# The first two tiles are only centred, their deviation moves behind the first product, and two context loads wait for gathered rows

## The chip, the core and the metric

The kernel runs on one core of a Trainium2 chip. Five engines work side by side, each through its own list of instructions in order: TensorE (PE in the profile) for matrix products, VectorE (DVE), ScalarE (ACT), GpSimd (POOL) and SyncE (SP), which here only issues transfers. The metric is the device time of one execution in microseconds, as the median of several runs: 421.14 us before (three runs, 420.02 to 422.06). All cores but one are idle, so the slowest core is the only one.

## The reference

`x` has 2048 rows (tokens) of 512. Two sub-layers follow each other:

```python
x = x + tanh(g_xattn) * moe(layernorm(x), token_ids, ctx, ctx, ctx)
x = x + tanh(g_ffn)   * ffn(layernorm(x), w_gate, w_up, w_down)
# moe: expert = min(clip(id, 0, 24999) // 6250, 3); per token, with C = ctx[expert] (512 x 512)
#      h = x @ C.T ; y = (silu(h) * h) @ C        (Wg, Wu and Wd are one and the same matrix)
# ffn: int8 activations, ternary weights, silu(gate) * up, a Walsh-Hadamard transform of 2048,
#      int8 again, and the product with w_down
# layernorm(x) = (x - mean) / sqrt(var + 1e-5), without weights
```

Because a row is only scaled by its deviation, `layernorm(x) @ C.T` is `((x - mean) @ C.T) * rstd`, where `rstd` is 1 / sqrt(var + 1e-5). The change rests on that.

## The kernel before

Tokens are sorted by expert. 16 tiles of 128 sorted rows are gathered from `x` by indirect transfers into `xs`; a tile that holds rows of two experts is computed once for each, so there are 19 items. An item goes through: `stats` (mean and variance, VectorE), `item_scale` (two GpSimd instructions: variance plus epsilon, then the power -1/2), `normalise` (VectorE, into `xn`), `x_transposes` (TensorE), `x_upper` and `x_lower` (the transposed tile is split in a high and a low part, ScalarE and VectorE), `up_product` (12 matmuls of high and low parts), `silu_h` (ScalarE), `act_mul` (VectorE), `a_transposes`, `a_upper` and `a_lower` (the same split), `down_product` (12 matmuls) and `update` (VectorE adds into `xs`). The context matrices are split too: `ct_upper(e)` on ScalarE and `ct_lower(e)` on VectorE, each over 128 x 2048. The first two items (`k < FIRST`, FIRST is 2) do without the split in the up product: `first_product` multiplies whole float32 values of `stage`, the buffer into which the four context matrices are loaded.

Beside the items, the weights of the second sub-layer are loaded into the same four slots of `stage` (`W_DRAM`, L258 to L265), measured, rounded and clipped. A quarter of the first weight matrix may be loaded once `ct_lower` of that slot is done and both first products are. After the items come 16 feed-forward tiles, from about 150 us on, in a software pipeline.

The order on every engine is written out by hand, and waits are on semaphores that count. For the first items it is:

- SP: constants, three context loads at once, the fourth (`e == E - 1`, L254) when the second gathered tile is in (`gathered[1]`), then the weights.
- POOL: gathers 0 to 2, `item_scale(0)`, `item_scale(1)`, gathers 3 to 6, `item_scale(2)`, `item_scale(3)`, gathers 7 to 10, and so on (L325 to L337). A gather's descriptors are made by GpSimd, so each gather occupies it.
- DVE (L1094 to L1115): the list that the change reorders; it is printed below.
- ACT: `ct_upper` of 0, 1 and 2, `x_upper(0)`, `x_upper(1)`, `ct_upper(3)`, `silu_h(0)`, `a_upper(0)`, then item by item.
- PE (L501 to L511): `spin` (matmuls whose result nobody reads, so that TensorE isn't idle), `x_transposes(0)`, `first_product(0)` with `x_transposes(1)` in its middle, `first_product(1)` with `a_transposes(0)` in its middle, `x_transposes(2)`, `down_product(0)`, `a_transposes(1)`, and then for every item k from 2: `up_product(k)`, `x_transposes(k + 1)`, `down_product(k - 1)`, `a_transposes(k)`.

`xn` has two buffers (`b = k % 2`), `item_rstd` and `item_mv` too; `sil`, `act`, `ps_aT` and `aT_hi`/`aT_lo` have one.

Of the kernel before, what the change touches and what calls it, by code (L numbers as in the profile page):

```python
# [75 lines left out]
def gated_moe_bitnet_kernel(nc, x, ids, ctxt, wgate, wup, wdown, gates, consts, out):  # L76
    with ExitStack() as persistent:
# [29 lines left out]
        item_rstd = sb("item_rstd", [P, 2], F32)  # L107
        ffn_stats = sb("ffn_stats", [P, 2, 6], F32)
# [106 lines left out]
        tables_set, tanh_done = sem("tables_set"), sem("tanh_done")  # L215
        ct_hi_set, ct_lo_set = sem("ct_hi_set"), sem("ct_lo_set")
# [31 lines left out]
        def _(sp):  # L248
# [4 lines left out]
            for e in range(E):  # L253
                if e == E - 1:  # L254
                    sp.wait_ge(gathered[1], 16)
                sp.dma_start(stage[:, e, :], ctxt[:, e, :]).then_inc(in_slot[e], 16)
# [45 lines left out]
        def _(pool):  # L302
# [11 lines left out]
            def item_scale(k, n):  # L314
# [6 lines left out]
                nc.gpsimd.tensor_tensor(item_rstd[:, b:b + 1], item_var[:, b:b + 1], neg_half[:, :],  # L321
# [98 lines left out]
        def _(pe):  # L420
# [44 lines left out]
            def first_product(k, between=None):  # L465

                e = expert_of(k)
                pe.wait_ge(ct_hi_set, e + 1)
# [32 lines left out]
            spin(18)  # L501
            pe.wait_ge(stats_set, 1)
            spin(5)
            x_transposes(0, 0)
            spin(4)
# [200 lines left out]
        def _(act_e):  # L706
# [20 lines left out]
            def silu_h(k):  # L727
                act_e.wait_ge(h_done, k + 1)
                nc.scalar.activation(sil, (first_h[k] if k < FIRST else ps_h)[:, :], ACT.Silu).then_inc(sil_set, 1)
# [20 lines left out]
            for e in range(E - 1):  # L750
                ct_upper(e)
            x_upper(0, 0)
            x_upper(1, 1)
            ct_upper(E - 1)
            silu_h(0)
            a_upper(0)
# [22 lines left out]
            for k in range(1, NI):  # L779
                w, i = k // 5, k % 5  # L780
                silu_h(k)
                if k + 1 < NI:
                    x_upper(k + 1, 1 - k % 2)
# [159 lines left out]
        def _(dve):  # L943
# [132 lines left out]

            def x_lower(k, b):
                dve.wait_ge(xT_hi_set, k + 1)
                tt(xT_lo[:, :], ps_xT[:, :], xT_hi[:, :].bitcast(F32), ALU.subtract).then_inc(xT_lo_set, 1)

            def act_mul(k):
                dve.wait_ge(sil_set, k + 1)
                tt(act, (first_h[k] if k < FIRST else ps_h)[:, :], sil, ALU.mult).then_inc(act_set, 1)
# [11 lines left out]
            stats(0, 0, st)  # L1095
            dve.wait_ge(gathered[1], 16)
            stats(1, 1, st)
            normalise(0, 0)
            normalise(1, 1)
            ct_lower(0)  # L1100
            ct_lower(1)
            act_mul(0)
            dve.wait_ge(gathered[2], 16)
            stats(2, 0, st)
            a_lower(0)
            normalise(2, 0)
            dve.wait_ge(gathered[3], 16)
            stats(3, 1, st)
# [392 lines left out]
```

## Time and profile before

| what | value |
|---|---|
| median of three runs | 421.14 us |
| lowest and highest | 420.02 and 422.06 us |
| the profiled execution's own time | 422.38 us |
| its span in the profile | 420.4 us |
| busy: PE, DVE, ACT, POOL | 390.6 us (93%), 365.4 us (87%), 291.2 us (69%), 178.7 us (43%) |
| first 20 us: PE, DVE, POOL busy | 9.88, 12.82, 6.04 us |
| 50 to 130 us: PE busy | 79.45 of 80 us |
| granted TensorE clock, mean | 0.996 |

The span is the time from the first to the last instruction of the profiled execution; the 1.98 us between it and that execution's time lie outside what the profile shows. TensorE is busy 93% of the span, and nearly all of the time from 50 to 130 us. In the first 20 us it is busy for less than half, and much of that are spins. So the start is a stretch with another limit than the rest. In the rows further below, L numbers are lines of the kernel before; `bank` is a PSUM bank; "scratch" stands for `xn`, `sil` or `act`, which are parts of it; `wq` in the first 30 us is where the whole transposed first tiles lie (`xT_whole`).

### The profile page before, as it was taken

The page shows a single profiled execution, that of the slowest core. Times are in us where ns is not written, and L with a number is a line of the kernel's source. Part 1 is how long each engine was busy: PE and PEld are TensorE (multiplying, and loading weights), DVE is VectorE, ACT ScalarE, POOL GpSimd, SP SyncE. Part 2 cuts the span into 40 slices and gives each one's busy share as a digit, 9 for nine tenths or more (in the row PEclk, how much of TensorE's full clock was granted, in tenths as well). Part 3 has the DMA queues.
Part 4 walks back from the last instruction along what each step waited for, and adds up shares of the span by engine and source line. Part 5 has one row for each costly group of instructions (what it writes and reads, how often), then busy time and mean ns, then how long its engine had stood idle before and what let it go on. Part 6 is the DMA issues. An engine that isn't in the chain of part 4 may idle for free.

```text
span 420.4 us, 7393 instructions
## 1 busy us (share of the span) xinstructions
PE 390.6 (93%) x2203; PEld 270.0 (64%) x2203; DVE 365.4 (87%) x652; ACT 291.2 (69%) x450; POOL 178.7 (43%) x208
## 2 busy tenths in 40 slices
PE   1899999999999999988999999999999999999891
PEld 0347788888887664755666666666666666667740
DVE  5788587679885889999999999999999999998980
ACT  4446686687784343667878878878878878877960
POOL 0667311014123202174475575575575575522021
PEclk9999999999999999999999999999999999999998
DMA  7759474065000001336255245255155155155241
GB/s 257 251 160 410 157 247 154 1 212 189 2 13 2 0 14 38 39 62 90 50 101 126 49 103 126 46 108 125 42 112 125 38 112 125 39 113 114 50 101 50
DMA packets 48968, 43.66 MB, mean 104 GB/s; under 512 B 42672, under 2 KB 42800, under 8 KB 46896
## 3 DMA queue, kind: packets, MB, share of 16 engines
q1 hardware_dynamic: 44224, 27.11, 23.4%
q0 software_dynamic: 4720, 16.26, 16.3%
q8 instruction: 13, 0.21, 0.2%
q14 instruction: 11, 0.09, 0.1%
HBM read 21.33 MB, written 4.19 MB: 61 GB/s over the span
## 4 chain that ended last, share of the span: by engine, by line
PE 77%; DVE 11%; issue 5%; DMA 4%; ACT 1%; POOL 0%; DVEq 0%; SPq 0%; POOLq 0%; ACTq 0%
PE bank L461 21%; PE bank L584 12%; PE bank L591 11%; PE bank L560 10%; PE bank L567 10%; PE bank L423 9%; DVE prod L1174 2%; DVE mixed L1201 1%; DVE ct_lo L964 1%; DMA xqT<-xq 1%; DMA xs<-x_dram,order 1%; PE bank L528 1%; DVE prod L1201 1%; PE bank L677 1%; DMA yqT<-yq 1%
## 5 line engine op out<-in xcount | busy, mean ns | idle before, releaser
L584 PEld LDWEIGHTS bank<-cst,mT 128*128 128x128 f32 x512 | 66.3, 191 | 14.1 <-issue 2.7
L584 PE MATMUL bank<-cst,mT 128*128 128x128 f32 x512 | 67.8, 276 | 4.0 <-ACT mT L829 4.0
L560 PE MATMUL bank<-wq,xqT 128*128 128x512 bf16 x240 | 61.6, 379 | 1.7 <-DMA xqT<-xq 1.7
L591 PE MATMUL bank<-wq,yqT 128*128 128x512 bf16 x240 | 61.3, 379 | 0.7 <-DMA yqT<-yq 0.7
L567 PE MATMUL bank<-wq,xqT 128*128 128x512 bf16 x240 | 61.6, 379 | 0.0
L829 ACT ACTIVATE mT<-bank 128x512 f32<-128x512 f32 x64 | 37.6, 592 | 18.4 <-PE bank L423 18.4
L406 POOL DMA_INDIRECT out_dram<-res,order x16 | 19.5, 1217 | 70.8 <-DVE res L1295 70.8
L817 ACT ACTIVATE y<-y,yqs 128x512 int8<-128x512 f32 x56 | 40.2, 717 | 9.9 <-POOL yqs L366 9.9
L854 ACT ACTIVATE sg<-bank,gate_s 128x512 f32<-128x512 f32 x60 | 41.0, 683 | 7.4 <-PE bank L560 7.2
L1174 DVE TENSOR_TENSOR prod<-bank,sg 128x512 f32<-128x512 f32 x64 | 43.4, 677 | 1.1 <-ACT sg L854 0.8
L834 ACT ACTIVATE y<-bank 128x512 f32<-128x512 f32 x64 | 37.6, 588 | 8.8 <-PE bank L584 8.6
L567 PEld LDWEIGHTS bank<-wq,xqT 128*128 128x128 bf16 x240 | 23.5, 98 | 28.3
L423 PE MATMUL bank<-cst,mixed 128*128 128x128 f32 x256 | 37.9, 273 | 0.2 <-DVE mixed L1193 0.2
L1274 DVE TENSOR_REDUCE ymax_part<-y 128x1 f32<-128x1024 f32 x30 | 36.3, 1211 | 2.1 <-ACT y L834 1.1
L423 PEld LDWEIGHTS bank<-cst,mixed 128*128 128x128 f32 x256 | 31.5, 141 | 10.2 <-issue 0.4
L1201 DVE TENSOR_TENSOR mixed<-prod 128x1024 f32<-128x1024 f32 x32 | 37.9, 1219 | 0.1
L1201 DVE TENSOR_TENSOR prod<-bfly 128x1024 f32<-128x1024 f32 x30 | 36.0, 1211 | 0.0
L822 ACT ACTIVATE yq<-y 128x512 bf16<-128x512 int8 x56 | 35.2, 629 | 0.6
L1201 DVE TENSOR_TENSOR bfly<-prod 128x1024 f32<-128x1024 f32 x30 | 35.3, 1217 | 0.0
L364 POOL TENSOR_SCALAR out_s<-yamax,down_c 128x1 f32<-128x1 f32 x13 | 28.6, 2197 | 15.6 <-DVE yamax L1285 15.6
L560 PEld LDWEIGHTS bank<-wq,xqT 128*128 128x128 bf16 x240 | 23.1, 98 | 18.3 <-issue 2.7
L591 PEld LDWEIGHTS bank<-wq,yqT 128*128 128x128 bf16 x240 | 23.1, 98 | 17.2 <-DMA yqT<-yq 1.1
(154 smaller groups left out, 810.2 us busy)
## 6 DMA issues: line engine op xcount, KB each, us to landing
mixed<-mixed POOLq DMA_DIRECT2D x15, 512.0 KB, 5.3
stage<-ctx_dram SPq DMA_DIRECT2D x4, 1024.0 KB, 7.5
stage<-wgate_dram SPq DMA_DIRECT2D x4, 1024.0 KB, 8.5
stage<-wup_dram SPq DMA_DIRECT2D x4, 1024.0 KB, 4.7
stage<-wdown_dram SPq DMA_DIRECT2D x4, 1024.0 KB, 4.7
yqT<-yq SPq DMA_TRANSPOSE x60, 2.4
cst<-consts_dram SPq DMA_DIRECT2D x1, 274.0 KB, 3.3
xs<-x_dram,order POOLq DMA_INDIRECT x16, 4.2
```

The costliest lines, as they stand in the source:

```text
L423: last = nc.tensor.transpose(bank_[:, c * P:(c + 1) * P], src(c), ident)
L461: last = nc.tensor.matmul(bank_[:, :], l[:, cols], r[:, ds(e * DC + c), :], start=(c == 0 and n == 0), stop=(c == DC - 1 and n == 2))
L560: last = nc.tensor.matmul(ps_gate[:, :], xqT[:, b, c, :], wq[:, 0, c * F + 512 * n:c * F + 512 * (n + 1)], start=(c == 0), stop=(c == DC - 1))
L567: last = nc.tensor.matmul(ps_up[n % 2][:, :], xqT[:, b, c, :], wq[:, 1, c * F + 512 * n:c * F + 512 * (n + 1)], start=(c == 0), stop=(c == ...
L584: last = nc.tensor.matmul(bank_[:, c * P:(c + 1) * P], mT[:, n % 2, c, :], had, start=True, stop=True)
L591: last = nc.tensor.matmul(ps_down[b][:, :], yqT[:, m, g, :], wq[:, 2, block_ * D:(block_ + 1) * D], start=(m == 0 and g == 0), stop=(m == ...
L817: nc.scalar.activation(y8[:, m % 2, :], y[:, b, 512 * m:512 * (m + 1)], ACT.Copy, scale=yqs[:, b:b + 1]).then_inc(yround_set, 1)
L829: nc.scalar.activation(mT[:, n % 2, :, :].rearrange("p c m -> p (c m)"), ps_mT[n % 2][:, :], ACT.Copy).then_inc(mT_set, 1)
L834: nc.scalar.activation(y[:, b, 512 * n:512 * (n + 1)], bank_[:, :], ACT.Copy).then_inc(y_set, 1)
L854: nc.scalar.activation(sg[:, n % 2, :], ps_gate[:, :], ACT.Silu, scale=gate_s[:, b:b + 1]).then_inc(sg_set, 1)
L1174: tt(prod[:, b, 4 * n:4 * n + 4, :].rearrange("p c m -> p (c m)"), up[n % 2][:, :], sg[:, n % 2, :], ALU.mult).then_inc(prod_set, 1)
L1201: return tt(dst[:, :, half], src[:, :, 0], src[:, :, 1], ALU.subtract if half else ALU.add)
```

## The change

- `normalise(0)` and `normalise(1)` are replaced by `centre(0)` and `centre(1)`, which subtract the mean and wait for no deviation. The deviation (now in a buffer of its own, `first_rstd`) is applied as the scale of the Silu and as a scalar in `act_mul`, of the first two items only. `centre(0)` now stands before `stats(1)`.
- On VectorE, `stats(2)` moves ahead of `act_mul(0)`, `normalise(2)` ahead of `a_lower(0)`, and `ct_lower(1)` from before `act_mul(0)` to between `normalise(2)` and `a_lower(0)`. Two waits for `rstd_set` are added ahead of `stats(2)` and `stats(3)`.
- The third context matrix is loaded when the first gathered tile is in, the fourth when the third is.
- On ScalarE, a new semaphore `ctx_in` tells TensorE that a context matrix has arrived. `ct_upper(2)` moves from before `x_upper(0)` to behind `silu_h(0)`, and `ct_upper(3)` from before `silu_h(0)` to behind `x_upper(2)`; ScalarE waits for both arrivals before `silu_h(0)`.
- The spins: 18, a wait for the first statistics, 5 and 4 become 20 and 3.
- The GpSimd order stays as it was.

```diff
--- before.py
+++ after.py
@@ -251,8 +253,10 @@
             sp.dma_start(cst[:, C_RANK:C_N], consts[:, C_RANK:C_N]).then_inc(in_small, 16)
             sp.dma_start(gate_in[:, :], gates).then_inc(in_gate, 16)
             for e in range(E):
-                if e == E - 1:
-                    sp.wait_ge(gathered[1], 16)
+                if e == 2:
+                    sp.wait_ge(gathered[0], 16)
+                if e == 3:
+                    sp.wait_ge(gathered[2], 16)
                 sp.dma_start(stage[:, e, :], ctxt[:, e, :]).then_inc(in_slot[e], 16)
 
             for w in range(3):
@@ -318,7 +322,8 @@
                 nc.gpsimd.tensor_scalar(item_var[:, b:b + 1], item_mv[:, b, 1:2], 1.0, LN_EPS, ALU.mult,
                                         ALU.add).then_inc(pool_step, 1)
                 pool.wait_ge(pool_step, n + 1)
-                nc.gpsimd.tensor_tensor(item_rstd[:, b:b + 1], item_var[:, b:b + 1], neg_half[:, :],
+                rstd = first_rstd if k < FIRST else item_rstd
+                nc.gpsimd.tensor_tensor(rstd[:, b:b + 1], item_var[:, b:b + 1], neg_half[:, :],
                                         ALU.pow).then_inc(rstd_set, 1)
                 return n + 1
 
@@ -465,7 +470,7 @@
             def first_product(k, between=None):
 
                 e = expert_of(k)
-                pe.wait_ge(ct_hi_set, e + 1)
+                pe.wait_ge(ctx_in, e + 1)
                 pe.wait_ge(xT_hi_set, k + 1)
                 for c in range(DC):
                     if c == DC // 2 and between is not None:
@@ -498,11 +503,9 @@
                 pe.wait_ge(aT_lo_set, k + 1)
                 product(bank_, aT_hi[:, :], aT_lo[:, :], e, y_done)
 
-            spin(18)
-            pe.wait_ge(stats_set, 1)
-            spin(5)
+            spin(20)
             x_transposes(0, 0)
-            spin(4)
+            spin(3)
             pe.wait_ge(tables_set, 1)
             first_product(0, lambda: x_transposes(1, 1))
             first_product(1, lambda: a_transposes(0))
@@ -726,7 +729,12 @@
 
             def silu_h(k):
                 act_e.wait_ge(h_done, k + 1)
-                nc.scalar.activation(sil, (first_h[k] if k < FIRST else ps_h)[:, :], ACT.Silu).then_inc(sil_set, 1)
+                if k < FIRST:
+                    act_e.wait_ge(rstd_set, k + 1)
+                    nc.scalar.activation(sil, first_h[k][:, :], ACT.Silu,
+                                         scale=first_rstd[:, k:k + 1]).then_inc(sil_set, 1)
+                else:
+                    nc.scalar.activation(sil, ps_h[:, :], ACT.Silu).then_inc(sil_set, 1)
 
             def a_upper(k):
                 act_e.wait_ge(aT_done, k + 1)
@@ -747,12 +755,20 @@
                 nc.scalar.activation(w8(w, c), stage[:, c, :], ACT.Copy,
                                      scale=wscale[:, w:w + 1]).then_inc(wround_set, 1)
 
-            for e in range(E - 1):
+            def ctx_arrived(e):
+
+                act_e.wait_ge(in_slot[e], 16)
+                nc.scalar.nop().then_inc(ctx_in, 1)
+
+            for e in range(2):
+                ctx_arrived(e)
                 ct_upper(e)
             x_upper(0, 0)
             x_upper(1, 1)
-            ct_upper(E - 1)
+            ctx_arrived(2)
+            ctx_arrived(3)
             silu_h(0)
+            ct_upper(2)
             a_upper(0)
 
             def ln_normalise(t, b):
@@ -779,7 +795,10 @@
             for k in range(1, NI):
                 w, i = k // 5, k % 5
                 silu_h(k)
-                if k + 1 < NI:
+                if k == 1:
+                    x_upper(2, 0)
+                    ct_upper(3)
+                elif k + 1 < NI:
                     x_upper(k + 1, 1 - k % 2)
                 if w < 3 and i in (2, 3):
                     weight_abs(w, 2 * i - 3)
@@ -1074,13 +1093,20 @@
                 ts(xn[:, b, :], rows(tau), item_mv[:, b, 0:1], item_rstd[:, b:b + 1], ALU.subtract,
                    ALU.mult).then_inc(xn_set, 1)
 
+            def centre(k, b):
+                dve.wait_ge(stats_set, k + 1)
+                ts(xn[:, b, :], rows(k), item_mv[:, b, 0:1], None, ALU.subtract).then_inc(xn_set, 1)
+
             def x_lower(k, b):
                 dve.wait_ge(xT_hi_set, k + 1)
                 tt(xT_lo[:, :], ps_xT[:, :], xT_hi[:, :].bitcast(F32), ALU.subtract).then_inc(xT_lo_set, 1)
 
             def act_mul(k):
                 dve.wait_ge(sil_set, k + 1)
-                tt(act, (first_h[k] if k < FIRST else ps_h)[:, :], sil, ALU.mult).then_inc(act_set, 1)
+                if k < FIRST:
+                    stt(act, first_h[k][:, :], first_rstd[:, k:k + 1], sil, ALU.mult, ALU.mult).then_inc(act_set, 1)
+                else:
+                    tt(act, ps_h[:, :], sil, ALU.mult).then_inc(act_set, 1)
 
             def a_lower(k):
                 dve.wait_ge(aT_hi_set, k + 1)
@@ -1093,18 +1119,20 @@
 
             dve.wait_ge(gathered[0], 16)
             stats(0, 0, st)
+            centre(0, 0)
             dve.wait_ge(gathered[1], 16)
             stats(1, 1, st)
-            normalise(0, 0)
-            normalise(1, 1)
+            centre(1, 1)
             ct_lower(0)
+            dve.wait_ge(gathered[2], 16)
+            dve.wait_ge(rstd_set, 1)
+            stats(2, 0, st)
+            act_mul(0)
+            normalise(2, 0)
             ct_lower(1)
-            act_mul(0)
-            dve.wait_ge(gathered[2], 16)
-            stats(2, 0, st)
             a_lower(0)
-            normalise(2, 0)
             dve.wait_ge(gathered[3], 16)
+            dve.wait_ge(rstd_set, 2)
             stats(3, 1, st)
             act_mul(1)
             x_lower(2, 0)
```

## Rows read from the trace of the kernel before

**Rows 1.** The page, the chain that ended last: shares of the span by engine.

```profile
PE 77%; DVE 11%; issue 5%; DMA 4%; ACT 1%; POOL 0%; DVEq 0%; SPq 0%; POOLq 0%; ACTq 0%
```

**Rows 2.** The chain of waits from 0 to 60 us: start us, us, what.

```profile
12.72 4.24 DMA xs<-x_dram,order
...
22.98 1.80 ACT ct_hi L719
...
30.50 4.49 DVE ct_lo L964 x2
...
36.95 3.03 PE bank L461 x12
```

**Rows 3.** Timeline, VectorE, first tiles: start, duration, engine, line, out<-in [idle before<-releaser].

```profile
16.98 0.69 DVE L1065 BATCH_NORM_STATS2 item_stats<-xs 128x6 f32<-128x512 f32 x1 [1.03 <-DMA xs<-x_dram,order]
17.71 0.18 DVE L1068 BATCH_NORM_AGGREGATE item_mv<-item_stats 128x2 f32<-128x6 f32 x1
...
17.81 0.53 DVE L1074 TENSOR_SCALAR scratch<-xs,item_mv,item_rstd 128x512 f32<-128x512 f32 x1
...
19.57 4.48 DVE L964 TENSOR_TENSOR ct_lo<-stage,ct_hi 128x2048 fp32r<-128x2048 f32 x2
...
25.30 0.69 DVE L1083 TENSOR_TENSOR scratch<-bank,scratch 128x512 f32<-128x512 f32 x1 [1.24 <-ACT scratch L729]
...
27.36 0.69 DVE L1087 TENSOR_TENSOR aT_lo<-bank,aT_hi 128x512 fp32r<-128x512 f32 x1 [0.56 <-ACT aT_hi L733]
...
27.97 0.54 DVE L1074 TENSOR_SCALAR scratch<-xs,item_mv,item_rstd 128x512 f32<-128x512 f32 x1
28.42 0.69 DVE L1065 BATCH_NORM_STATS2 item_stats<-xs 128x6 f32<-128x512 f32 x1
```

**Rows 4.** Timeline, GpSimd, the same stretch.

```profile
17.98 0.41 POOL L318 TENSOR_SCALAR item_var<-item_mv 128x1 f32<-128x1 f32 x1 [1.09 <-DVE item_mv L1068]
18.47 0.56 POOL L321 TENSOR_TENSOR item_rstd<-item_var,neg_half 128x1 f32<-128x1 f32 x1
19.20 1.10 POOL L310 DMA_INDIRECT xs<-x_dram,order  x1 [0.17 <-issue]
20.61 2.15 POOL L310 DMA_INDIRECT xs<-x_dram,order  x1 [0.30 <-issue]
23.06 1.89 POOL L310 DMA_INDIRECT xs<-x_dram,order  x1 [0.30 <-issue]
25.25 1.01 POOL L310 DMA_INDIRECT xs<-x_dram,order  x1 [0.30 <-issue]
26.90 0.19 POOL L318 TENSOR_SCALAR item_var<-item_mv 128x1 f32<-128x1 f32 x1 [0.64 <-DVE item_mv L1068]
```

**Rows 5.** Timelines of GpSimd and of VectorE about 140 us.

```profile
140.70 1.61 POOL L346 TENSOR_TENSOR ffn_rstd<-ffn_var,neg_half 128x1 f32<-128x1 f32 x1
...
139.35 2.54 DVE L1160 TENSOR_SCALAR wq<-wq 128x2048 bf16<-128x2048 int8 x2
```

**Rows 6.** Landing times: gathers issued from 10 to 21 us, then context loads.

```profile
DMA to landing us min/median/max: 3.5/3.8/4.5
...
DMA to landing us min/median/max: 4.7/7.5/10.4
```

**Rows 7.** Timeline, TensorE: weight loads of spins, the first product, a later gap.

```profile
10.90 0.15 PEld L450 LDWEIGHTS bank<-cst 128*128 128x128 bf16 x1 [0.28 <-issue]
...
13.89 1.43 PEld L450 LDWEIGHTS bank<-cst 128*128 128x128 bf16 x7 [0.28 <-issue]
...
19.93 1.98 PE L473 MATMUL bank<-stage,wq 128*128 x4
...
196.03 1.03 PE L560 MATMUL bank<-wq,xqT 128*128 128x512 bf16 x4 [1.73 <-DMA xqT<-xq]
```

**Rows 8.** Waits after 36 us: who waited for whom, us in total, times, longest.

```profile
ACT wq L740 <- DMA stage<-wgate_dram: 1.1, 3, 0.5
...
PEld bank L549 <- ACT wq L740: 0.3, 1, 0.3
```

More of the change, by code:

```diff
@@ L107, in gated_moe_bitnet_kernel @@
         item_rstd = sb("item_rstd", [P, 2], F32)
+        first_rstd = sb("first_rstd", [P, 2], F32)
         ffn_stats = sb("ffn_stats", [P, 2, 6], F32)
@@ L215, in gated_moe_bitnet_kernel @@
         tables_set, tanh_done = sem("tables_set"), sem("tanh_done")
+        ctx_in = sem("ctx_in")
         ct_hi_set, ct_lo_set = sem("ct_hi_set"), sem("ct_lo_set")
```

## The prediction

> **What bounds the kernel now.** I read the page first, then the chain of waits from 0 to 60 us, then the timelines of VectorE and GpSimd side by side, and last the waits behind 36 us. On the page the chain that ended last is 77% TensorE [rows 1]. From the start of `down_product(1)` at 36.95 us TensorE works nearly without a gap through the items (79.45 of the 80 us from 50 to 130), so this start is the hinge: what moves it moves the end, and what doesn't move it is free. Ahead of it the chain passes from engine to engine [rows 2]: the landing of the second gathered tile, the fourth `ct_upper` (which stands in front of `silu_h(0)`), and then VectorE with `ct_lower(2)` and `ct_lower(3)`, 4.49 us. From `a_lower(0)` at 27.36 us on VectorE has no gap to speak of up to 36.95 [rows 3]. So VectorE's list, not TensorE's, sets the hinge.
>
> **The change part by part.**
>
> *Centring instead of normalising.* `normalise(0)` starts at 17.81 us because it stands behind `stats(1)` [rows 3]. `centre(0)` comes right behind `stats(0)`, some 1.9 us sooner, and the first product, now at 19.93 us [rows 7], can start as much sooner, near 18.0. That is the visible gain. It counts only if it reaches the hinge.
>
> *What VectorE still has to do.* No big instruction goes; they are reordered. Before, `ct_lower(0)` and `ct_lower(1)` run from 19.57 to 24.05 us, in time in which VectorE would otherwise wait for `silu_h(0)`: `act_mul(0)` comes 1.24 us after them [rows 3]. So `ct_lower(1)` is hidden now. In the change it stands behind `normalise(2)`, and `a_lower(0)` behind it. From the start of `normalise(2)`, called N, to `down_product(1)` there were 36.95 - 27.97 = 8.98 us. Now the same list holds one `ct_lower` more (4.48 / 2 = 2.24) and `a_lower(0)` (27.97 - 27.36 = 0.61), and `act_mul(1)` becomes an instruction with a scalar; the trace shows none on these operands, so I bound it by 0 and 0.2 and take 0.05. Together 11.88 us. The hinge is at N + 11.88, and it stays where it is only if N is 25.07 or less; today N is 27.97.
>
> *When can `normalise(2)` start?* It needs the deviation of the third tile, which GpSimd makes in `item_scale(2)`, and in GpSimd's list that stands behind gathers 3 to 6. Moving `stats(2)` up by 5 us doesn't change that order. So N is a sum on GpSimd:
> - The second tile lands at 16.98 as now. The three first gathers took 3.5 to 4.5 us to land [rows 6], so it could come 0.7 sooner with less other traffic, or 0.3 later; I keep it. `stats(1)` ends at 17.71 + 0.18 = 17.89 [rows 3], `centre(1)` starts at 17.93, and `ct_lower(0)` 0.45 behind (as 28.42 behind 27.97), at 18.38. It ends at about 20.65.
> - The small instruction of `item_scale(1)` took 0.41 instead of 0.19 us: it began inside `normalise(0)` and ended with it [rows 3, 4]. With `centre(1)` in that place it ends near 18.4, and the power starts at about 18.5, within `ct_lower(0)`. In [rows 5] the same form of power began inside two VectorE instructions of 2.54 us and lasted 1.61 us instead of 0.56: it ended 0.42 us after they did. So the deviation of item 1 comes at 20.65 + 0.42 = 21.07, two microseconds later than now (18.47 + 0.56).
> - Gather 3 starts 0.17 later, at 21.24. A gather outside a `ct_lower` lasts 1.01 to 1.10 us with 0.30 in between, while two that began inside one took 2.15 and 1.89 [rows 4]. In the change all four run clear of one: three spacings of 1.36 and the last 1.01 give 21.24 + 4.08 + 1.01 = 26.33. Then 0.08, the variance 0.19, 0.08, the power 0.56 and 0.03 to VectorE: N = 27.3.
>
> The hinge moves to 27.3 + 11.88 = 39.2, later by 2.2 us. In words: the early start of the first product is lost in a wait of VectorE for GpSimd, from `act_mul(0)` (done near 24.4) to 27.3, and `ct_lower(1)`, which used to fill such a wait, now comes after it.
>
> A rule of the Trainium skill bears on the gathers. The trace shows gathers begun inside `ct_lower` at 2.15 and 1.89 us beside 1.01 [rows 4]. The page "SBUF — State Buffer", section "Who interferes with whom", says that a VectorE instruction with two SBUF inputs holds up a GpSimd instruction that reads SBUF, and infers that the making of descriptors is not held up. By the first half the power waits, as summed; by the second the gathers here wouldn't be held, against the trace. For the sum it makes no difference as long as the power waits, since no gather then begins inside a `ct_lower`; it decides in the third rival.
>
> *Context loads.* The third now leaves at about 15 us instead of 3.5, and the fourth when tile 2 is in, about 18. Landing took 4.7 us for the one that had the engines nearly to itself and 10.4 at most [rows 6]. So the fourth arrives at about 23, and `silu_h(0)` (which waits for both) starts there instead of at 24.7. `act_mul(0)` is over at 24.4, 2.9 us ahead of N: hidden. If that cover is gone, each microsecond beyond an arrival at 25.9 costs one. `ct_upper(2)` ends near 25.6 and `ct_upper(3)` near 31, both ahead of the `ct_lower` that reads them: nothing. The wait blocks SP's list, but behind it stand only the weight loads, which may leave only after both first products.
>
> *Weights.* The first quarter of the first weight matrix leaves at about 27 instead of 28.5, the others 1 to 2 us later than now. ScalarE waits 1.1 us in all for these landings, and TensorE 0.3 us for ScalarE [rows 8]. With less to land at once some of that goes: 0 to 0.3, I take 0.15.
>
> *Spins.* 27 become 23, all ahead of 18 us in waiting time: nothing, if TensorE keeps its clock (second rival).
>
> **The sum.** 2.2 - 0.15, rounded: 2.1 us later, from the hinge to the end, since TensorE takes up everything behind it. Against the profiled execution (span 420.4, own time 422.38) that is a span of 422.5 and a time of 424.5. The profiled execution was 1.24 us above the median of the runs, 421.14, and the shift is the same for both: 423.2.
>
> The bounds of the unknown costs: N may come 0.7 sooner (landing) or 0.5 later (a landing 0.3 later and 0.2 in the gathers), `act_mul` 0 to 0.2, weights 0 to 0.3. That makes +1.2 to +2.9 about the likeliest case: 422.3 to 424.0.
>
> **The rivals.**
> 1. *The fourth context matrix lands late.* It shares the engines with gathers 2 to 4. At the longest landing [rows 6] it comes at 18.3 + 10.4 = 28.7, `act_mul(0)` ends at 30.0, the hinge is at 41.9: +4.9, 426.0. For it: that wait stands in front of every later ScalarE step. Against it: the 10.4 us belong to a load queued behind two others, while this one has at most one ahead. Chance 7%.
> 2. *TensorE's clock falls.* Between `first_product(1)` (ends near 26.9) and `down_product(0)` (starts near 31.0) TensorE now has only the 0.5 us of `x_transposes(2)`. The profile gives a mean granted clock of 0.996, yet early spins stand 0.15 + 0.28 = 0.43 us apart and later ones 1.43 / 7 = 0.20 [rows 7], for 512 columns the 1.2 and the 2.4 GHz level. After 16 us the longest gap is 1.73 us [rows 7], and the spacing stays short behind it, so the trace can't rule it out. The slow stretch at the start lasts about 4 us, in which ten matmuls pass; with `down_product(0)` in such a stretch `down_product(1)` would come about 0.7 us later than by VectorE, and 2.4 if all that follows were slow too. I take 1: +3.1, 424.2. Chance 12%. The Trainium skill, "TensorE: Matmul & The Clock Gate", section "HAM oscillation — how this bites in real kernels", describes clocks that fall in waits between bursts of matmuls.
> 3. *The power slips in ahead of `ct_lower(0)`.* The two start within 0.1 us of each other. Then gather 3 starts at 19.2 as now, inside `ct_lower(0)`, and as in [rows 4] ends 0.9 behind it, at 21.6; N = 26.6, +1.4, 422.5. Chance 14%. If gathers begun inside a `ct_lower` weren't held up either, N = 25.2 and the hinge moves by 0.1: 421.2. Chance 5%. That is what the page named above infers of them.
> 4. *Faster: the early start carries through.* If the deviation of the third tile were there when `act_mul(0)` ends, at 24.4, the hinge would be at 36.3, and with a still earlier landing and fewer waits of ScalarE the full 1.9 us of the first product could reach the end: -0.7 to -1.9 us, 419.2 at best. The point that decides is N = 25.07. Against it: four gathers of 1.36 us from 19.2 on alone pass it. Chance 8%.
> 5. *The rest, 2%*: the stretch behind the hinge absorbs the shift.
>
> **How the numbers follow.** The likeliest case has 52%. What a measurement here can tell from no change is about 0.5%, 2.1 us, and the forecast lies on that edge: half of its chance is slower (26%), half the same (26%). Slower also take rivals 1 and 2 (19%): 45%, and 1 more for the spread of the runs. Same: 26 + 14 + 5 + 2 from the likeliest case, rival 3 and the rest, and 2 of rival 4: 49%. Faster: rival 4 alone stays below 2.1 us and needs the spread of the runs besides; I give it 5% of its 8, and 1 to slower. The range takes in rival 3 with both its ends and rival 2, and leaves out most of rivals 1 and 4: 421.0 to 424.7.
>
> **What would show it.** Right: `centre(0)` near 16, the first product near 18; the power of item 1 over 1.5 us long; VectorE idle ahead of `normalise(2)` with GpSimd's deviation as releaser, N at 27.3; `ct_lower(1)` behind it; `down_product(0)` near 31 instead of 29.57 and `down_product(1)` near 39.2. Wrong: gathers 3 to 6 that start before 20.6, N below 26, `silu_h(0)` after 26, or matmuls of `down_product(0)` 0.43 us apart.

## The result, and the profile after

| | before | after |
|---|---|---|
| median of six runs each | 421.10 us (420.02 to 422.06) | 423.73 us (422.96 to 424.57) |
| the profiled execution's own time | 422.38 us | 423.42 us |
| its span | 420.4 us | 421.5 us |
| granted TensorE clock, mean | 0.996 | 0.988 |

After / before is 1.0062, with a 95% interval of 1.0045 to 1.0079: slower by 2.6 us. (The 421.14 us further up is the median of the first three of the six runs.) The forecast was 423.2 us in a range of 421.0 to 424.7.

The constants land at 4.1 us in one profile and at 3.4 in the other, and everything shifts with them. So all times below that are called "behind the order" are counted from the VectorE instruction that writes `order`, the first on which the gathers rest. In the profile before it starts here (timeline, VectorE; start, duration, engine, line, out<-in):

```profile
10.09 0.17 DVE L1004 SCALAR_TENSOR_TENSOR order<-order_part 128x16 int32<-128x16 f32 x1
```

The timeline of the kernel after, all engines, from the order to the first weight sums:

```profile
9.40 0.17 DVE L1023 SCALAR_TENSOR_TENSOR order<-order_part 128x16 int32<-128x16 f32 x1
...
15.23 0.49 DVE L1098 TENSOR_SCALAR scratch<-xs,item_mv 128x512 f32<-128x512 f32 x1
...
17.31 1.98 PE L478 MATMUL bank<-stage,wq 128*128 x4 [0.23 <-ACT wq L727]
...
17.72 2.28 DVE L983 TENSOR_TENSOR ct_lo<-stage,ct_hi 128x2048 fp32r<-128x2048 f32 x1
...
17.94 2.48 POOL L326 TENSOR_TENSOR first_rstd<-item_var,neg_half 128x1 f32<-128x1 f32 x1
...
20.59 1.10 POOL L314 DMA_INDIRECT xs<-x_dram,order  x1 [0.17 <-issue]
...
24.64 0.69 ACT L734 ACTIVATE scratch<-bank,first_rstd 128x512 f32<-128x512 f32 x1 [4.28 <-DMA stage<-ctx_dram]
...
25.36 0.75 DVE L1107 SCALAR_TENSOR_TENSOR scratch<-bank,first_rstd,scratch 128x512 f32<-128x512 f32 x1 [4.53 <-ACT scratch L734]
...
26.00 0.57 POOL L326 TENSOR_TENSOR item_rstd<-item_var,neg_half 128x1 f32<-128x1 f32 x1
...
26.17 1.12 PE L428 MATMUL bank<-cst,scratch 128*128 128x128 f32 x4 [3.00 <-DVE scratch L1107]
26.61 0.55 DVE L1093 TENSOR_SCALAR scratch<-xs,item_mv,item_rstd 128x512 f32<-128x512 f32 x1 [0.50 <-POOL item_rstd L326]
...
27.07 2.29 DVE L983 TENSOR_TENSOR ct_lo<-stage,ct_hi 128x2048 fp32r<-128x2048 f32 x1
27.07 2.95 PE L478 MATMUL bank<-stage,wq 128*128 x4
...
29.27 0.69 DVE L1113 TENSOR_TENSOR aT_lo<-bank,aT_hi 128x512 fp32r<-128x512 f32 x1
...
30.11 6.77 SPq L269 DMA_DIRECT2D stage<-wgate_dram  x4
...
38.50 0.49 PE L466 MATMUL bank<-ct_hi,aT_hi 128*128 x1 [0.58 <-DVE aT_lo L1113]
...
49.09 0.39 PE L552 MATMUL bank<-wabs,cst 128*128 128x4 f32 x2 [0.73 <-ACT wq L748]
```

What to see, against [rows 3, 4, 7]: the first product starts at 17.31 instead of 19.93, behind the order 7.91 instead of 9.84, so 1.9 us sooner. The power of item 1 (`first_rstd`, 17.94) begins 0.22 us inside `ct_lower(0)` and lasts 2.48 us instead of 0.56. The four gathers behind it take 1.01 to 1.10 each, none is held. `item_rstd` of the third tile is over at 26.57, and `normalise(2)` (26.61) waited 0.50 for it. `ct_lower(1)` (27.07) comes behind it, then `a_lower(0)` (29.27). `down_product(1)`, the hinge, starts at 38.50: behind the order 29.10, before 36.95 - 10.09 = 26.86, so 2.24 later.

Two things in these lines were not in the likeliest case of the forecast. `silu_h(0)` (24.64) waited 4.28 us for a context matrix, and TensorE, which had nothing to do for 3.00 us, did the four transposes at 26.17 in 1.12 us instead of 0.66, and the second half of `first_product(1)` in 2.95 instead of 1.88. The same two in the profile before:

```profile
26.04 0.66 PE L423 MATMUL bank<-cst,scratch 128*128 128x128 f32 x4 [0.26 <-DVE scratch L1083]
26.54 1.88 PE L473 MATMUL bank<-stage,wq 128*128 x4
```

The loads of the first weights can only leave behind that product; they leave at 30.11, and at 49.09 TensorE waits 0.73 us for the sums of these weights. The stages show the clock (columns: stretch, length, busy time of PE, PEld, DVE, ACT and POOL with instruction counts, granted clock, share of the DMA engines, GB/s):

```profile
20.00:40.00 20.00, 15.64 (x59) 10.14 (x58) 14.89 (x21) 10.44 (x13) 12.04 (x13) 0.91 0.77 280
...
27.00:28.00 1.00, 1.00 (x4) 0.48 (x3) 1.00 (x2) 0.72 (x2) 0.00 (x0) 0.50 0.47 184
```

Before it is 1.00 from 20 to 40 us, with TensorE busy for 18.66 of the 20 us. Here it is 0.50, the lower of the two levels (1.2 instead of 2.4 GHz), from 26.2 to 29.0 us. The waits of the first 60 us (who for whom: us in total, times, longest) answer to [rows 8]:

```profile
ACT wq L748 <- DMA stage<-wgate_dram: 3.2, 4, 1.1
...
PEld bank L552 <- ACT wq L748: 1.0, 1, 1.0
```

ScalarE waits 3.2 us for landings of the weights instead of 1.1. The chain of waits of the same stretch, from the third gather on, has three transfers on it:

```profile
13.36 6.21 DMA xs<-x_dram,order
19.59 4.88 DMA stage<-ctx_dram
...
36.55 10.46 DMA stage<-wgate_dram
```

The third gather needed 6.21 us to land, where the three first gathers before took 3.7 to 4.2: the third context matrix, which left at 14.21, shared the DMA engines with it. All kernels bear that out: the third gather took 6.2 to 6.9 us in the five that load the third matrix just behind it (after, e1, e4, e5, e6 below), and 3.7 to 4.0 in the eight profiles with the loads as before. Only then could the fourth leave. Behind the order the fourth arrived at 24.47 - 9.40 = 15.07. The last line is the last quarter of the first weights, from its issue to its landing.

### The profile page after: what moved, and what is told of

It is laid out like the page before. It is cut to its first block, busy times and chain, and to the rows that moved or that the text cites. A ratio compares the mean times of both kernels' runs of the same rounds, so it can differ in the third digit from the quotient of the medians.

```text
span 421.5 us, 7358 instructions
## 1 busy us (share of the span) xinstructions
PE 387.9 (92%) x2166; PEld 270.5 (64%) x2199; DVE 365.2 (87%) x652; ACT 291.2 (69%) x450; POOL 179.1 (43%) x208
## 3 DMA queue, kind: packets, MB, share of 16 engines
q1 hardware_dynamic: 44224, 27.11, 24.4%
## 4 chain that ended last, share of the span: by engine, by line
PE 70%; DMA 9%; DVE 9%; issue 5%; ACT 4%; POOL 1%; DVEq 0%; SPq 0%; POOLq 0%; ACTq 0%
PE bank L466 19%; PE bank L587 11%; PE bank L594 10%; PE bank L563 9%; PE bank L570 9%; PE bank L428 8%; DMA yqT<-yq 4%; DMA stage<-wgate_dram 2%; DVE prod L1202 2%; DMA xs<-x_dram,order 1%; DMA stage<-ctx_dram 1%; ACT y L836 1%; PE bank L531 1%; DVE prod L1229 1%; PE bank L680 1%
## 5 line engine op out<-in xcount | busy, mean ns | idle before, releaser
L594 PE MATMUL bank<-wq,yqT 128*128 128x512 bf16 x227 | 59.1, 379 | 2.5 <-DMA yqT<-yq 1.7
L570 PE MATMUL bank<-wq,xqT 128*128 128x512 bf16 x232 | 61.0, 379 | 0.4
L563 PE MATMUL bank<-wq,xqT 128*128 128x512 bf16 x231 | 59.8, 379 | 0.5
L570 PEld LDWEIGHTS bank<-wq,xqT 128*128 128x128 bf16 x240 | 23.5, 98 | 28.3
L369 POOL TENSOR_SCALAR out_s<-yamax,down_c 128x1 f32<-128x1 f32 x13 | 29.7, 2283 | 15.0 <-DVE yamax L1313 15.0
```

The lines of the kernel that those rows point to most:

```text
L563: last = nc.tensor.matmul(ps_gate[:, :], xqT[:, b, c, :], wq[:, 0, c * F + 512 * n:c * F + 512 * (n + 1)], start=(c == 0), stop=(c == DC - 1))
L570: last = nc.tensor.matmul(ps_up[n % 2][:, :], xqT[:, b, c, :], wq[:, 1, c * F + 512 * n:c * F + 512 * (n + 1)], start=(c == 0), stop=(c == ...
L594: last = nc.tensor.matmul(ps_down[b][:, :], yqT[:, m, g, :], wq[:, 2, block_ * D:(block_ + 1) * D], start=(m == 0 and g == 0), stop=(m == ...
```

## Experiments

Behind the order, in us. N is the start of `normalise(2)`, "up 4" that of `up_product(4)`, the first that stands behind the weight sums on TensorE; "sums" is what TensorE (its weight load, where that is longer) waited ahead of them. A ratio compares runs of one series, and the median of the kernel before was 421.10, 420.61, 420.57 and 420.54 us in the four series (after; e1 to e4; e5 to e8; e3_again and e10), so kernels of different series are compared here by ratio.

| kernel | N | hinge | up 4 | sums | median us | ratio to before, 95% |
|---|---|---|---|---|---|---|
| before | 17.88 | 26.86 | 37.76 | 0.3 | 421.1 | |
| e9_before_again | 18.37 | 27.35 | 38.21 | 0.2 | (420.44 once) | |
| after | 17.21 | 29.10 | 40.67 | 1.0 | 423.73 | 1.0062 (1.0045 to 1.0079) |
| e1_gpsimd_order | 16.99 | 29.50 | 40.67 | 0.6 | 423.00 | 1.0053 (1.0032 to 1.0074) |
| e2_loads_as_before | 17.35 | 29.13 | 39.58 | 0 | 422.79 | 1.0050 (1.0034 to 1.0066) |
| e3_both | 13.62 | 25.44 | 35.70 | 0 | 418.49 | 0.9953 (0.9936 to 0.9970) |
| e3_again | 13.73 | 25.64 | 36.03 | 0 | 418.49 | 0.9950 (0.9929 to 0.9971) |
| e4_ct_lower_back | 19.06 | 29.67 | 40.37 | 0 | 423.55 | 1.0072 (1.0055 to 1.0089) |
| e5_spins | 17.14 | 28.91 | 39.17 | 0 | 422.26 | 1.0038 (1.0025 to 1.0051) |
| e6_gpsimd_and_spins | 17.25 | 29.00 | 39.29 | 0 | 422.93 | 1.0041 (1.0024 to 1.0058) |
| e7_centring_alone | 18.78 | 28.35 | 38.61 | 0 | 420.76 | 1.0006 (0.9988 to 1.0023) |
| e8_both_ct3_late | 14.34 | 25.29 | 37.86 | 2.0 | 420.04 | 0.9996 (0.9976 to 1.0016) |
| e10_ct1_in_gap | 14.68 | 25.51 | 38.13 | 2.0 | 421.07 | 1.0001 (0.9983 to 1.0020) |

### Does GpSimd's order hold normalise(2), or the loads?

**e1_gpsimd_order**, the deviation of the third tile right behind gather 3:

```diff
-            for t in range(3, 7):
-                gather(t)
-            n = item_scale(2, n)
+            gather(3)
+            n = item_scale(2, n)
+            for t in range(4, 7):
+                gather(t)
             n = item_scale(3, n)
```

> The changed kernel, with one edit: on GpSimd item_scale(2) stands behind gather 3 instead of behind gather 6. The hinge is counted from the VectorE instruction that writes order to the start of down_product(1): 26.86 us before (36.95 - 10.09), 29.10 in the changed kernel (38.50 - 9.40). Theory A (the loss is VectorE's wait for the third tile's deviation, with ct_lower(1) behind it): the deviation is there 3 us sooner, but normalise(2) then waits for act_mul(0), which ends at 26.1 because the fourth context matrix arrives at 24.5; so the hinge gains only about 0.5 us, 28.6, and the time is 423.2. Theory B (the loss is the late context loads and the clock that falls behind them): nothing changes, 423.7.

**e2_loads_as_before**, the context loads of the kernel before:

```diff
-                if e == 2:
-                    sp.wait_ge(gathered[0], 16)
                 if e == 3:
-                    sp.wait_ge(gathered[2], 16)
+                    sp.wait_ge(gathered[1], 16)
```

> The changed kernel, with the context loads issued as before the change (three at once, the fourth when tile 1 is in). Theory A: silu_h(0) starts near 21.7 instead of 24.6, TensorE no longer idles 3 us inside first_product(1) and its matmuls stand 0.43 apart again, but normalise(2) still waits for GpSimd until 26.6: the hinge stays at 29.1. The first weight quarter leaves near 27 instead of 30.1, and TensorE's wait of 1.0 us for the absolute sums shrinks to about 0.3: 0.7 us in all, 423.0. Theory B: the whole loss of 2.6 us goes, 421.1.

**e3_both** is e1 and e2 together.

> Both edits together: item_scale(2) behind gather 3, and the context loads as before the change. Theory A: act_mul(0) is over near 23.1 and the deviation of the third tile is there near 22.8, so normalise(2) starts near 23.1 instead of 26.6; the hinge comes 3.5 us sooner than in the changed kernel, 25.6 behind order, and with 0.7 us less wait for the weights the time is about 419.5, 1.6 us below before. Theory B: as with the loads alone, 421.1.

Alone, neither moves N by more than 0.22 us. Each removes one of two waits that end nearly together. The timeline of e1 (its order at 9.56):

```profile
22.25 0.57 POOL L326 TENSOR_TENSOR item_rstd<-item_var,neg_half 128x1 f32<-128x1 f32 x1
...
25.17 0.69 ACT L735 ACTIVATE scratch<-bank,first_rstd 128x512 f32<-128x512 f32 x1 [4.83 <-DMA stage<-ctx_dram]
...
25.89 0.75 DVE L1108 SCALAR_TENSOR_TENSOR scratch<-bank,first_rstd,scratch 128x512 f32<-128x512 f32 x1 [4.84 <-ACT scratch L735]
26.55 0.54 DVE L1094 TENSOR_SCALAR scratch<-xs,item_mv,item_rstd 128x512 f32<-128x512 f32 x1
...
31.34 0.75 DVE L1108 SCALAR_TENSOR_TENSOR scratch<-bank,first_rstd,scratch 128x512 f32<-128x512 f32 x1 [0.63 <-ACT scratch L735]
```

The deviation is there at 22.82, but `act_mul(0)` (25.89) stands ahead of `normalise(2)` and waits, by way of `silu_h(0)`, for the fourth context matrix. And `act_mul(1)` (31.34) waits 0.63 for its Silu, since TensorE had been slow as in the kernel after (the four products took 3.40 us). So the hinge came 0.4 later instead of the 0.5 sooner that I expected; e6 below takes that wait away. In e2 it is the other way round (order at 9.76):

```profile
23.29 0.75 DVE L1105 SCALAR_TENSOR_TENSOR scratch<-bank,first_rstd,scratch 128x512 f32<-128x512 f32 x1 [1.95 <-ACT scratch L732]
...
27.11 0.55 DVE L1091 TENSOR_SCALAR scratch<-xs,item_mv,item_rstd 128x512 f32<-128x512 f32 x1 [3.08 <-POOL item_rstd L324]
```

`act_mul(0)` is over at 24.04, and `normalise(2)` then waits 3.08 us for GpSimd. With both edits (order at 9.29):

```profile
22.25 0.75 DVE L1106 SCALAR_TENSOR_TENSOR scratch<-bank,first_rstd,scratch 128x512 f32<-128x512 f32 x1 [1.16 <-ACT scratch L733]
22.30 0.57 POOL L324 TENSOR_TENSOR item_rstd<-item_var,neg_half 128x1 f32<-128x1 f32 x1
22.91 0.59 DVE L1092 TENSOR_SCALAR scratch<-xs,item_mv,item_rstd 128x512 f32<-128x512 f32 x1
...
34.73 0.49 PE L465 MATMUL bank<-ct_hi,aT_hi 128*128 x1 [0.55 <-DVE aT_lo L1112]
```

N falls by 3.6 us and the hinge with it, to 25.44 behind the order, 1.4 ahead of the first profile of the kernel before and 1.9 ahead of the second. The clock stays at 1.00 from 20 to 40 us. This kernel beats both: 418.49 us, 0.5% under the kernel before. A second series gave the same:

> The version with item_scale(2) behind gather 3 and the context loads as before the change, once more, beside the next one. As the first time: 0.5% below before, 418.5, hinge at 25.4 behind order and up_product(4) at 35.7.

### Was it the place of ct_lower(1)?

**e4_ct_lower_back** puts it back behind `ct_lower(0)`, all else as after:

```diff
             ct_lower(0)
+            ct_lower(1)
...
             normalise(2, 0)
-            ct_lower(1)
             a_lower(0)
```

> The changed kernel, with ct_lower(1) back in its old place, directly behind ct_lower(0), and so no longer between normalise(2) and a_lower(0). Theory A: 2.24 us leave the chain behind normalise(2), but the power of item 1 on GpSimd now begins inside two ct_lower in a row and is held until 0.42 us behind the second, 4.7 us long instead of 2.5; gathers 3 to 6 and the deviation of the third tile come 2.2 us later, normalise(2) at 28.8: the hinge stays at 29.0 to 29.1, time 423.7. Rival C (the order on VectorE alone counts, GpSimd isn't held by a second instruction): the power ends where it did, and the hinge comes 2.2 us sooner, 26.9, time 421.5.

N came later and the list behind it got shorter. The power was held by the first `ct_lower` alone, not by both as I had expected, and gather 3 by the second (order at 9.30):

```profile
18.20 2.48 POOL L326 TENSOR_TENSOR first_rstd<-item_var,neg_half 128x1 f32<-128x1 f32 x1
...
20.86 2.60 POOL L314 DMA_INDIRECT xs<-x_dram,order  x1 [0.17 <-issue]
...
28.36 0.55 DVE L1093 TENSOR_SCALAR scratch<-xs,item_mv,item_rstd 128x512 f32<-128x512 f32 x1 [2.00 <-POOL item_rstd L326]
...
31.24 0.75 DVE L1107 SCALAR_TENSOR_TENSOR scratch<-bank,first_rstd,scratch 128x512 f32<-128x512 f32 x1 [0.91 <-ACT scratch L734]
```

Then `act_mul(1)` waited 0.91 us for its Silu, and the hinge ended at 29.67, no better. If VectorE's order alone had made the loss (the rival in the expectation), it would have been at 26.9. Where `ct_lower(1)` stands doesn't decide while GpSimd and the fourth context matrix set N.

### What did TensorE's pause cost?

**e5_spins** fills it, 13 spins ahead of `a_transposes(0)` inside `first_product(1)`:

```diff
+            def filled():
+                spin(13)
+                a_transposes(0)
+
-            first_product(1, lambda: a_transposes(0))
+            first_product(1, filled)
```

> The changed kernel with 13 more spins (matmuls of 512 columns that nobody reads) in the middle of first_product(1), ahead of a_transposes(0), where TensorE idles 3 us. Theory A: the second half of first_product(1) runs with matmuls 0.43 apart instead of 0.86 and ends 1.3 us sooner (28.7 instead of 30.0), but act_mul(1) has other VectorE work in front of it, so the hinge stays at 29.1 behind order; only the weight quarters leave sooner and TensorE's wait for the absolute sums shrinks, 0.3 to 0.7 us: 423.2. Theory D (the clock that falls is a good part of the loss): 1.3 us less, 422.4.

**e6_gpsimd_and_spins** is the same on e1.

> The changed kernel with item_scale(2) behind gather 3 and the same 13 spins. With the GpSimd edit alone the hinge did not come sooner (29.50 behind order) although normalise(2) did: act_mul(1) waited 0.63 us for silu_h(1), whose product ran at half the spacing after a gap of 3.5 us. Theory A: with the spins that wait goes, and the hinge is at 28.9; with less wait for the weights the time is 0.8 us below the changed kernel, 422.6. If the clock isn't what delayed silu_h(1), the hinge stays at 29.5.

The timeline of e5 (TensorE and the weight loads):

```profile
23.06 2.97 PE L455 MATMUL bank<-cst 128*128 128x512 bf16 x13
...
26.41 0.66 PE L428 MATMUL bank<-cst,scratch 128*128 128x128 f32 x4 [0.39 <-DVE scratch L1112]
...
26.90 1.88 PE L478 MATMUL bank<-stage,wq 128*128 x4
...
28.88 7.80 SPq L269 DMA_DIRECT2D stage<-wgate_dram  x4
```

The four transposes take 0.66 us and the four products 1.88 again, the granted clock from 20 to 40 us is 1.00, and the weight loads leave at 28.88 - 9.39 = 19.49 behind the order instead of 20.71. The hinge moved by only 0.19 us, `up_product(4)` by 1.50, and TensorE no longer waits for the weight sums. Between e1 and e6 the hinge moved by 0.50, since `act_mul(1)` no longer waits for its Silu, and `up_product(4)` by 1.38. By their ratios e5 is 1.0 us faster than after and e6 0.5 faster than e1, with intervals that overlap in both pairs: the profiles show the mechanism, the times at most its direction and no size.

The clock also fell elsewhere. In e2, which has no pause inside `first_product(1)`, TensorE waited 1.25 us ahead of `x_transposes(2)` and 2.35 ahead of `down_product(0)`, and within that product the clock went to the lower level (last but two: granted clock):

```profile
32.00:34.80 2.80, 2.80 (x8) 2.08 (x7) 2.80 (x3) 0.00 (x0) 2.32 (x3) 0.52 0.92 351
```

`down_product(0)` took 4.15 us there (30.72 to 34.87) instead of 2.85, but TensorE was still through with the next product 0.1 us before `a_lower(1)` let it go on, so it cost nothing at the hinge.

### Centring alone

**e7_centring_alone**: `centre`, the scale in the Silu and the scalar in `act_mul`; loads, ScalarE's and VectorE's orders as before. Of VectorE's list:

```diff
             centre(1, 1)
             ct_lower(0)
-            dve.wait_ge(gathered[2], 16)
-            dve.wait_ge(rstd_set, 1)
-            stats(2, 0, st)
+            ct_lower(1)
             act_mul(0)
-            normalise(2, 0)
-            ct_lower(1)
+            dve.wait_ge(gathered[2], 16)
+            dve.wait_ge(rstd_set, 1)
+            stats(2, 0, st)
             a_lower(0)
+            normalise(2, 0)
```

> The centring and the deferred deviation alone: context loads, ScalarE's order and VectorE's order (ct_lower(0) and ct_lower(1) in a row, stats(2) behind act_mul(0), a_lower(0) ahead of normalise(2)) as in the kernel before, spins as in the changed one. Theory A: the first product starts 1.9 us sooner and act_mul(0) about 1 us sooner, but ct_lower(0) also starts 1.1 us sooner, ahead of the power of item 1; the power is held for 2.5 us, gather 3 by ct_lower(1) until 0.9 behind it, and the third tile's deviation comes near 18.7 behind order, 0.9 later than normalise(2) started before: hinge 27.7 instead of 26.86, time 0.8 above before, 421.7. Rival C (VectorE's order is the whole loss): 1 us below before, 419.8.

The timeline (order at 9.28):

```profile
17.90 2.48 POOL L324 TENSOR_TENSOR first_rstd<-item_var,neg_half 128x1 f32<-128x1 f32 x1
...
20.55 2.60 POOL L312 DMA_INDIRECT xs<-x_dram,order  x1 [0.17 <-issue]
...
28.06 0.55 DVE L1085 TENSOR_SCALAR scratch<-xs,item_mv,item_rstd 128x512 f32<-128x512 f32 x1 [1.73 <-POOL item_rstd L324]
```

The early start of the first product buys nothing here either: the power waits for the first `ct_lower`, gather 3 for the second, and N is 18.78 where it was 17.88. By VectorE the hinge would be at 27.8 (`a_lower(1)` starts at 36.11, and the hinge is 0.94 behind it in e5), as I expected, but it was at 28.35. TensorE had waited 1.97 us ahead of `x_transposes(2)`, and most of `down_product(0)` ran at the lower clock, 4.44 us instead of 2.85; from there to the hinge TensorE had no gap:

```profile
30.60:33.80 3.20, 3.20 (x9) 2.41 (x9) 3.20 (x3) 0.00 (x0) 2.87 (x2) 0.50 1.02 413
...
37.63 0.48 PE L464 MATMUL bank<-ct_hi,aT_hi 128*128 x1
```

So the clock set this hinge, 0.6 us behind VectorE's. "Up 4" is 0.9 late against the first profile of the kernel before and 0.4 against the second. In time 420.76 stands beside 420.57 of the kernel before, an interval of -0.5 to +1.0 us: it neither shows nor excludes the 0.8 us that I expected.

### Two tries to go on from e3

**e8_both_ct3_late**: e3 with `ct_lower(3)` behind `a_lower(1)`. **e10_ct1_in_gap**: e3 with `ct_lower(1)` ahead of `act_mul(0)`.

```diff
 e8          ct_lower(2)
-            ct_lower(3)
             normalise(3, 1)
             update(0)
             a_lower(1)
+            ct_lower(3)
 e10         stats(2, 0, st)
+            ct_lower(1)
             act_mul(0)
             normalise(2, 0)
-            ct_lower(1)
             a_lower(0)
```

> A version meant to be faster: the changed kernel with item_scale(2) behind gather 3, the context loads as before, and ct_lower(3) moved from ahead of normalise(3) to behind a_lower(1). In the version without the last edit VectorE has no gap from act_mul(0) to the hinge at 25.44 behind order. Taking 2.24 us out of that list leaves TensorE's own work as the bound: up_product(2) starts at 21.4, takes 3.2 with the transposes, so the hinge is at 24.8 to 24.9, 0.6 sooner: 418.0. If ct_lower(3) then holds up up_product(3), nothing is gained, 418.5.

> The same version with ct_lower(1) moved from behind normalise(2) to ahead of act_mul(0), into VectorE's gap of 1.2 us there. The chain behind normalise(2) loses 2.24 us, but act_mul(0) starts 1.1 us later, item_scale(2) on GpSimd now begins inside ct_lower(1) and is held until its end, so normalise(2) starts near 14.9 behind order instead of 13.6, and act_mul(1) has to wait about 0.6 us for silu_h(1): hinge between 24.6 and 25.3 instead of 25.4. Theory A: 0.1 to 0.8 us faster, 418.1. If the hold didn't matter, 1.1 us: 417.4.

Both missed, by 2.0 and 3.0 us. In e8 `normalise(3)` waited 0.46 us for GpSimd, and the late `ct_lower(3)` freed the fourth slot of `stage` late; TensorE waited for the weights:

```profile
31.75 0.60 DVE L1092 TENSOR_SCALAR scratch<-xs,item_mv,item_rstd 128x512 f32<-128x512 f32 x1 [0.46 <-POOL item_rstd L324]
...
44.19 1.91 ACT L747 ACTIVATE wq<-stage 128x2048 bf16<-128x2048 f32 x1 [1.66 <-DMA stage<-wgate_dram]
...
46.24 0.38 PE L551 MATMUL bank<-wabs,cst 128*128 128x4 f32 x2 [1.75 <-ACT wq L747]
```

In e10 the second `ct_lower` held `item_var` of the third tile for 1.29 us, and each of the four quarters of the weights came late for ScalarE, which waited 5.4 us for them in all:

```profile
22.29 1.29 POOL L320 TENSOR_SCALAR item_var<-item_mv 128x1 f32<-128x1 f32 x1
...
32.55 1.91 ACT L747 ACTIVATE wq<-stage 128x2048 bf16<-128x2048 f32 x1 [1.68 <-DMA stage<-wgate_dram]
...
46.75 0.39 PE L551 MATMUL bank<-wabs,cst 128*128 128x4 f32 x2 [1.79 <-ACT wq L747]
```

In both the hinge stayed within 0.4 us of e3's, and 2.2 to 2.4 us were lost between it and `up_product(4)`. The last quarter left 23.6 us behind the order in e10 and 23.5 in e3, but ScalarE could begin on it only at 35.1, against 32.7. Why it took longer to land I did not settle. In e10 the clock fell too, behind the waits of 1.79 and 0.59 us around the weight sums, so that `up_product(4)` itself took 4.43 us instead of 2.86:

```profile
48.00:52.00 4.00, 4.00 (x12) 3.13 (x12) 0.32 (x2) 0.00 (x0) 0.00 (x0) 0.57 0.01 4
```

### How much does one profile tell?

**e9_before_again** is the kernel before, unchanged, to see whether the 1.73 us wait for `xqT` at 196 us [rows 7] belongs to it.

> The kernel before, unchanged, for a second profile. In its first profile TensorE waits 1.73 us at 194 us for a transposing transfer, which neither the changed kernel nor any experiment shows, and the execution took 422.4 us beside a median of 421.1. If that wait is chance, it is absent here, the hinge is 26.9 behind order, the start of up_product(4) 37.8, and the span 1 to 2 us shorter than 420.4. If it belongs to the kernel before, it is here again, and the changed kernel gets 1.7 us back there.

Its span is 418.5 us, 1.9 shorter, and it does not wait there. e5 and e6 have such a wait (1.75 and 1.53 us), the kernel after and the others not. So it comes and goes with the execution, and it is why the spans of the first two profiles differ by only 1.1 us and the medians by 2.6. The same kernel's hinge moved by 0.49 us between its two profiles, N with it: differences of that size between single profiles say nothing. Against this second profile the kernel after is 1.75 us late at the hinge and 2.46 at `up_product(4)`.

From `up_product(4)` to the end of the span eight of the thirteen profiles take 370.8 to 371.0 us, the kernel after 371.4; before, e5 and e6 take 372.6 to 373.0 with the wait for `xqT`, and e10 373.0 with its slow `up_product(4)`. So what an edit did up to `up_product(4)` nearly all reached the end.

## Why the prediction was right, and which steps weren't

In the profile before, the order stands 0.69 us later; forecasts are moved by it here.

- **Centring.** Right: the first product came 1.93 us sooner, forecast 1.9, and none of it reached the hinge.
- **The held power and the gathers.** Right: forecast at 21.07 for the end of the power, 21.24 for gather 3, 27.3 for N; measured 20.42, 20.59 and 26.61, with 0.69 added 21.11, 21.28 and 27.30. e1 to e3 show that this was the cause only together with the next point: remove one and N stays.
- **VectorE's list from N to the hinge.** Right: forecast 11.88 us, measured 38.50 - 26.61 = 11.89. `act_mul(1)` with a scalar took 0.75 instead of 0.66, but the instruction behind it started only 0.03 us later than it would have, where I had taken 0.05. Where nothing else waits the distance holds in the experiments too: 11.77 to 11.91 in e2, e3, e3_again, e5.
- **Context loads: the step mis-sized.** "The fourth arrives at about 23 ... `act_mul(0)` is over at 24.4, 2.9 us ahead of N: hidden." It arrived at 24.47 + 0.69 = 25.16, and `act_mul(0)` was over at 26.11 + 0.69 = 26.80, 0.5 ahead of N. The cause was the third gather, whose landing I had kept at up to 4.5 us and which took 6.21. The first rival put this lateness at the wrong place (the load's own landing, 4.88 us, was near its shortest). It cost nothing at the hinge (29.13 in e2, 29.10 in the kernel after), but it is why e1 alone gained nothing, and why TensorE stood idle for 3.00 us, which delayed the weights (next point).
- **Weights: the term that was wrong in sign.** I took -0.15. From the hinge to `up_product(4)` it was 11.57 us instead of 10.90, +0.67. I had the first product of item 1 over at 26.9 and the loads leaving at 27; they left at 30.11 + 0.69 = 30.8. In e5 and e2, where they leave sooner, the same stretch is 10.26 and 10.45 us, that is -0.64 and -0.45: the sign of my term is right where TensorE isn't delayed.
- **Clock rival: half right.** "Between `first_product(1)` and `down_product(0)`" was the wrong place for this kernel, though in e2 and e7 the clock fell just there. The pause came inside `first_product(1)`, 3.00 us long, and the matmuls behind it ran at the lower level, 1.2 GHz (their weight loads stand 0.85 us apart, 27.93 and 28.78, where those of the half before stand 0.43 apart; the granted clock is 0.50). `down_product(0)` ran at full pace, 0.23 us apart. At the hinge it cost 0.19 us (e5 against after; 0.50 in e6 against e1), about what two profiles of one kernel differ by (0.49), where I had priced 1; through the weights about 1.3 (1.50 at `up_product(4)` in e5, less 0.19). The Trainium skill, "TensorE: Matmul & The Clock Gate", section "HAM oscillation — how this bites in real kernels", describes clocks that fall in waits between bursts; the granted clock of 0.91 and the 2.95 us agree.
- **The power slips in ahead of `ct_lower(0)`.** It did so in no run: it began 0.21 to 0.22 us behind the start of `ct_lower(0)` in each.
- **The faster rival** was what e3 does: once the deviation is there when `act_mul(0)` ends, the hinge comes sooner. The reason I gave against it, four gathers in front of `item_scale(2)`, is what e1's edit removes; e2's edit has to come with it, since the late context matrix alone keeps N where it was.

The sum: +2.24 at the hinge and +0.67 behind it make 2.91 at `up_product(4)`, and 2.6 in the medians. I had 2.1. That the forecast was close rests on the hinge, not on the terms behind it, where the error was 0.8. The mechanism at the hinge is shown; that 2.2 was met to 0.04 is in part luck, since two profiles of the kernel before put their hinges 0.49 us apart.

## What to carry to other kernels

When an engine's list bounds the kernel, ask of each instruction at its head for all its inputs, and when each of them ends: here two ended within 0.5 us of each other, each edit alone gained nothing clear of the noise, and both together turned +0.6% into -0.5%. A small GpSimd operation that began inside a `ct_lower` lasted until its end, and everything queued behind it moved too, gathers above all. A wait of TensorE can cost twice: in six of these kernels (after, e1, e2, e4, e7, e10) matmuls behind it ran at half pace for a stretch, which cost nothing at the hinge in e2 and 0.6 us in e7. Delaying a load to relieve another is only a gain if what waits for it has slack; count from an event that all profiles share, and take a second profile before a difference of half a microsecond is given a meaning.

## What the runs showed of the hardware

- A power of one column on GpSimd that began inside a `ct_lower` of 2.28 us took 2.48 us instead of 0.57, in the changed kernel and all its variants, and ended 0.42 us behind it (20.00 and 20.42 in the kernel after). Gather 3, begun inside one, took 2.60 us (e4, e7) instead of 1.10. The Trainium skill, "SBUF — State Buffer", section "Who interferes with whom", states the first and infers that the making of descriptors is not held; for these gathers the runs disagree with the inference. An indirect gather also reads its row numbers (`order`) from SBUF, so the first half might cover it; no run separates the two.
- TensorE behind an idle stretch of 3.00 us did float32 matmuls at half pace (granted clock 0.50, 1.2 instead of 2.4 GHz) for about 3 us; with 13 spins in that stretch it did them at full pace. In e2 (waits of 1.25 and 2.35 us) and e10 (1.79 and 0.59) the clock fell only some matmuls into the product behind the waits.
- The gather of the third tile landed after 6.21 us where the 1 MB load of a context matrix had left 0.85 us behind it; in the eight profiles whose third context load had left long ahead, the same gather took 3.7 to 4.0.
